# Rewriting a delta-rule and expert kernel as straight-line code with raw keys, a 128-wide state, a second state in PSUM and predicated copies

## The reference, cut to what matters

```
z  = norm(x);  y = layernorm(z; dn_g, dn_b)
q, k, v = split(y @ gates_w + gates_b);  lr = y @ lr_w + lr_b
k  = k / |k|
A  = tril(k k^T, -1) + I;  u = solve_triangular(A, v, lower)      # per sequence, 1024 x 1024
h  = z + ((q k^T) @ (lr * u)) @ out_w + out_b                     # no causal mask
h  = h + relu(layernorm(h; mn_g, mn_b) @ w1 + b1) @ w2 + b2
x1 = x + h
e  = argmax(norm(x1) @ gate_w^T)                                  # 8 experts, one per position
out = x1 + norm(x1) + norm(x1) @ expert_w[e]^T
```

## Time and profile before

| | us |
|---|---|
| median of 3 runs (lowest, highest) | 296.16 (295.07, 334.09) |
| profiled execution, first to last instruction | 293.0 |
| PE busy | 211.6 (72%) |
| DVE busy | 208.1 (71%) |
| ACT busy | 153.6 (52%) |
| POOL busy | 104.6 (36%) |
| chain that ended last, by engine | PE 37%, DVE 35%, ACT 10%, issue 9% |

### The profile page before, as it was taken

The page is one execution under the profiler, slowest core; times in us unless marked ns, Lnnn a source line. Parts: engine busy times, 40 slices in busy tenths (PEclk is TensorE's granted clock), DMA queues, the critical chain, the costliest instruction groups (busy, mean ns, idle before and its releaser), DMA issues.

```text
span 293.0 us, 5160 instructions
## 1 busy us (share of the span) xinstructions
PE 211.6 (72%) x1322; PEld 143.6 (49%) x1322; DVE 208.1 (71%) x743; ACT 153.6 (52%) x466; POOL 104.6 (36%) x167
## 2 busy tenths in 40 slices
PE   0687678540007999999997362989798989897990
PEld 0475466330006888787873241736264544644440
DVE  5599997579993355555553425398989899999785
ACT  2578779630024555555531214275758685766851
POOL 6005455750000000000000503057576766867485
PEclk9979999855555899999999875799999999999997
DMA  5964454512002122222120100000110202010111
GB/s 121 254 220 178 158 233 166 232 67 115 0 1 107 38 110 96 86 110 80 58 112 2 37 36 0 0 1 24 51 33 38 72 2 72 0 38 0 36 36 36
DMA packets 18740, 22.39 MB, mean 76 GB/s; under 512 B 2328, under 2 KB 12576, under 8 KB 18720
## 3 DMA queue, kind: packets, MB, share of 16 engines
q1 hardware_dynamic: 18720, 22.16, 21.3%
HBM read 3.28 MB, written 2.10 MB: 18 GB/s over the span
## 4 chain that ended last, share of the span: by engine, by line
PE 37%; DVE 35%; ACT 10%; issue 9%; SPq 2%; DMA 2%; POOL 1%; DVEq 1%; ACTq 0%
PE ps L1019 8%; PE ps L1166 5%; PE ps L1025 4%; DVE xi L791 4%; DVE st L680 4%; PE ps L1159 4%; DVE prod L784 3%; PE ps L1236 3%; PE ps L1142 3%; ACT sq L464 3%; DVE xi L951 2%; DVE xnT L898 2%; DVE mv L687 2%; DVE lt L943 2%; PE ps L1252 2%
## 5 line engine op out<-in xcount | busy, mean ns | idle before, releaser
L1259 PE MATMUL ps<-ewT,tt 128*128 128x512 f32 x128 | 59.2, 599 | 1.6 <-DVE lt L943 1.4
L631 ACT ACTIVATE gd_all<-ps,oh 128x128 f32<-128x128 f32 x128 | 36.1, 368 | 18.2 <-PE ps L1259 15.7
L414 POOL TENSOR_TENSOR h_all<-h_all,cb 128x512 f32<-128x512 f32 (+1 forms) x8 | 10.2, 1270 | 95.8 <-DVE cb L871 95.8
L1259 PEld LDWEIGHTS ps<-ewT,tt 128*128 128x128 f32 x128 | 22.5, 190 | 27.4 <-issue 17.6
L951 DVE TENSOR_TENSOR xi<-lt,gd_all 128x512 f32<-128x512 f32 x32 | 25.4, 795 | 6.1 <-DVE lt L943 2.8
L230 POOL TENSOR_TENSOR xi<-xi 128x256 f32<-128x256 f32 x31 | 22.5, 726 | 16.0 <-DVE xi L951 16.0
L550 ACT COPY tt<-dT_all 32x128 f32<-32x128 f32 (+1 forms) x32 | 13.0, 407 | 23.2 <-DVE dT_all L796 22.7
L1092 PE MATMUL ps<-tt,gs 32*32 32x32 f32 x128 | 5.0, 203 | 27.2 <-ACT tt L550 26.5
L378 POOL COPY gd_all<-gg 32x128 f32 (+1 forms) x28 | 11.9, 425 | 31.6 <-ACT gg L482 28.6
L824 DVE TENSOR_TENSOR sm<-ps,sm 128x256 f32<-128x256 f32 x32 | 13.0, 421 | 12.9 <-PE ps L1166 12.4
L943 DVE TENSOR_TENSOR lt<-ps,oh 128x512 f32<-128x512 f32 x32 | 21.6, 676 | 0.0
(11 more groups left out here) (127 smaller groups left out, 497.3 us busy)
## 6 DMA issues: line engine op xcount, KB each, us to landing
kv_all<-kv SPq DMA_DIRECT2D x8, 512.0 KB, 3.1
kvs<-kv_all SPq DMA_DIRECT2D x8, 512.0 KB, 2.9
x_all<-in_L_attn_x_dram SPq DMA_DIRECT2D x8, 256.0 KB, 4.8
xnT_all<-xnT SPq DMA_DIRECT2D x8, 256.0 KB, 2.3
g_all<-gg SPq DMA_DIRECT2D x8, 256.0 KB, 2.3
gs<-g_all SPq DMA_DIRECT2D x8, 256.0 KB, 2.4
xns<-xnT_all SPq DMA_DIRECT2D x8, 256.0 KB, 2.4
out_dram<-x_all SPq DMA_DIRECT2D x8, 256.0 KB, 2.3
```

What stands on the lines that cost most here:

```text
L631: last = nc.scalar.activation(ea[b][:, e], ps[:, 4 + 2 * b, e * F:e * F + F], ACT.Copy, scale=oh[s][:, n, e:e + 1])
L1259: nc.tensor.matmul(ps[:, bank, :], zT[s][:, n], ewT[:, EH * half:EH * half + EH, :].rearrange("p e f -> p (e f)"), start=True, stop=True). ...
```

## The change

It does five things.

1. No loops: all tiles are unrolled in program order on each engine, every tile has its own place in SBUF (`kT_all`, `k_all`, `v_all`, `gg_all`, `tt_all`), and the DMAs into and out of the staging buffers go.
2. Raw keys: keys are not divided by their length. The transposed keys come straight from one matmul `wk` x xnT of 512 columns, and `k_` turns them back. The lengths come from the diagonal of the Gram blocks (`nkl`), the elimination works on scaled coefficients (`rd`, `lts`), and v is multiplied by the length in `rv_`.
3. State of 128 columns: `ks` applies S to the keys, `rv_` subtracts, `w_` multiplies by the inverse, `s_` makes k^T w of 128 columns. The second state is summed in PSUM bank 4 over all tiles by `m_`.
4. x1 is not normalized before the gate and the experts: their weights are centred (`cent`, `gwC`, `ewC`), x1 itself is turned, and the factor 1/sigma is applied at the end (`scale`). The outputs are chosen by one copy of the last expert (`default`, ACT) and 7 predicated copies (`pick`, DVE) for each pair of sequences; POOL adds the result (`add_`).
5. The orders are new. b2 is added after stage 1, and h (`h_`) is computed there too; POOL builds part of `tt` and `da` in stage 2.

```diff
-            def both(i, s):
-                diagonals(i, s)
-                plus_b2(i, s)
+        pool.wait_ge(ewT_ready, 1)
+        nc.gpsimd.tensor_tensor(ewT[:], ewT[:], ident[:, :].unsqueeze(1).broadcast_to([P, E, F]),
+                                ALU.add).then_inc(ewI_ready, 1)
+        pool.wait_ge(w_loaded, 16 * 10)
+        for t in range(T):
+            pool.wait_ge(h_ready, t + 1)
+            nc.gpsimd.tensor_tensor(x_all[:, t], x_all[:, t], b2s[:, :].unsqueeze(1).broadcast_to([P, NS, C]),
+                                    ALU.add).then_inc(xb2_ready, 1)
...
+        for t in range(T):
+            kT_(t)
+            if t + 2 < T:
+                root(t + 2)
+            if t + 1 < T:
+                xnT_(t + 1)
+            k_(t)
+            if t + 2 < T:
+                xh_(t + 2)
+            gg_(t)
...
+        nc.vector.reciprocal(rd[:], diagonal(lt)).then_inc(rd_done, 1)
+        nc.vector.tensor_tensor(lts[:], lt[:], rd[:].unsqueeze(1).broadcast_to([P, Q, Q]), ALU.mult).then_inc(elim, 1)
+        nc.vector.tensor_copy(diagonal(xi), rd[:]).then_inc(elim, 1)
...
-            nc.tensor.matmul(ps[:, 6 + n % 2, 0:2 * C], kvs[s][:, n, 0:C], uu[:, n], start=True,
-                             stop=True).then_inc(sm_mm[n][s], 1)
+        def ks(t, n):
+            pe.wait_ge(s_ready, (t - 1) * NS + n + 1)
+            nc.tensor.matmul(ps[:, n, 0:C], kT_all[:, t, n], sm[:, n], start=True, stop=True).then_inc(ks_mm, 1)
+        def w_(t, n):
+            pe.wait_ge(rv_ready, t * NS + n + 1)
+            if n == 0:
+                pe.wait_ge(t12_ready, t + 1)
+            nc.tensor.matmul(ps[:, n, C:2 * C], tt_all[:, t, n], rv[:, n], start=True, stop=True).then_inc(w_mm, 1)
+        def s_(t, n):
+            pe.wait_ge(w_ready, t * NS + n + 1)
+            nc.tensor.matmul(ps[:, n, 2 * C:3 * C], k_all[:, t, n], ww[:, n, 0:C], start=True, stop=True).then_inc(s_mm, 1)
+        def m_(t, n):
+            pe.wait_ge(lrw_ready, t * NS + n + 1)
+            last = nc.tensor.matmul(tiles(4)[:, n], ww[:, n, C:2 * C], k_all[:, t, n], start=t == 0 and n == 0,
+                                    stop=t == T - 1, skip_group_check=True)
...
-            nc.vector.tensor_tensor(ed[b], ps[:, 5 + 2 * b, :].rearrange("p (e f) -> p e f", e=EH),
-                                    oh[s][:, n, EH:E].unsqueeze(2).broadcast_to([P, EH, F]), ALU.mult).then_inc(ed_done[b], 1)
-            nc.vector.tensor_tensor(es[b], ed[b], ea[b], ALU.add).then_inc(sum_done[b], 1)
+        def default(t, pair):
+            act.wait_ge(ex_mm, 4 * t + 2 * pair + 1)
+            earlier(act, added, t - 1)
+            nc.scalar.copy(sel[t % 2][:, 2 * pair:2 * pair + 2], ps[:, 4:6, 0:F]).then_inc(default_set, 1)
+        def pick(t, pair, j):
+            e = j + 1
+            half = e // EH
+            b = 4 + 2 * half
+            n = slice(2 * pair, 2 * pair + 2)
+            if j == 0:
+                dve.wait_ge(mask_ready, t + 1)
+                dve.wait_ge(default_set, 2 * t + pair + 1)
+            else:
+                dve.wait_ge(picked, (E - 1) * (2 * t + pair) + j)
+            if j == 0 or e == EH:
+                dve.wait_ge(ex_mm, 4 * t + 2 * pair + half + 1)
+            nc.vector.copy_predicated(
+                sel[t % 2][:, n], mask[t % 2][:, n, E - 1 - e].unsqueeze(2).broadcast_to([P, 2, F]),
+                ps[:, b:b + 2, (e % EH) * F:(e % EH) * F + F]).then_inc(picked, 1)
+        def tn_(t, of):
+            act.wait_ge(hnb_done, t + 1)
...
+        def experts(t, pair, half):
+            i = 2 * t + pair
+            earlier(pe, picked, (E - 1) * i - (EH if half == 0 else 0))
+            for n in range(2):
+                last = nc.tensor.matmul(ps[:, 4 + 2 * half + n, :], x1T[t % 2][:, 2 * pair + n],
+                                        ewC[:, EH * half:EH * half + EH, :].rearrange("p e f -> p (e f)"),
+                                        start=True, stop=True)
+            last.then_inc(ex_mm, 1)
```

More of the change, by code:

```diff
@@ new lines, in xh_, with xnT_ @@
+            def xh_(t):
+                act.wait_ge(nb_done, t + 1)
+                earlier(act, xT_mm, t - 1)
+                for n in range(2, NS):
+                    last = nc.scalar.activation(xh[t % 2][:, n], x_all[:, t, n], ACT.Identity, bias=nb[:, t, 1, n:n + 1],
+                                                scale=rr[:, t, 1, n:n + 1])
+                last.then_inc(xh_act, 1)
+            def xnT_(t):
+                act.wait_ge(xT_mm, t + 1)
+                nc.scalar.activation(rows(xnT_all[:, t]), ps[:, 0, :], ACT.Identity, bias=dnb, scale=dng).then_inc(xnT_ready, 1)
@@ new lines, in _ @@
+            last.then_inc(tt_first, 1)
+            ya(0)
+            za(0)
+            y64_(0)
+            for t in range(T):
+                if t + 1 < T:
+                    ya(t + 1)
+                w_(t, 0)
+                w_(t, 1)
+                if t + 1 < T:
+                    za(t + 1)
+                w_(t, 2)
+                w_(t, 3)
+                lrw(t, 0)
+                lrw(t, 1)
+                if t + 1 < T:
+                    y64_(t + 1)
+                lrw(t, 2)
+                lrw(t, 3)
@@ new lines, in tT_, with hid_, x1T_ @@
+            def tT_(t):
+                act.wait_ge(tT_mm, t + 1)
+                earlier(act, hid_mm, t - 1)
+                nc.scalar.activation(rows(tT[t % 2]), ps[:, 1, :], ACT.Identity, bias=mnb, scale=mng).then_inc(tT_ready, 1)
+            def hid_(t):
+                act.wait_ge(hid_mm, t + 1)
+                earlier(act, out_mm, t - 1)
+                nc.scalar.activation(rows(hid[t % 2]), ps[:, 2, :], ACT.Relu, bias=b1c).then_inc(hid_ready, 1)
+            def x1T_(t):
+                act.wait_ge(x1T_mm, t + 1)
+                nc.scalar.copy(rows(x1T[t % 2]), ps[:, 1, :]).then_inc(x1T_ready, 1)
@@ L1014, in _ @@
-            pe.wait_ge(kvw_loaded, 16 * 6)
-            def four(bank, lhsT, rhs, ready, step=1):
-                for n in range(NS):
-                    last = nc.tensor.matmul(tiles(bank)[:, n], lhsT(n), rhs(n), start=True, stop=True)
-                last.then_inc(ready, step)
             def turn(bank, src, ready):
@@ new lines, in tT_, with hid_, out_ @@
+            def tT_(t):
+                pe.wait_ge(tn_ready, NS * (t + 1))
+                earlier(pe, x1T_ready, t)
+                turn(1, lambda n: tn[t % 2][:, n], tT_mm)
+            def hid_(t):
+                pe.wait_ge(tT_ready, t + 1)
+                earlier(pe, x1_ready, t)
+                nc.tensor.matmul(ps[:, 2, :], w1s[:], rows(tT[t % 2]), start=True, stop=True).then_inc(hid_mm, 1)
+            def out_(t):
+                pe.wait_ge(hid_ready, t + 1)
+                four(2, lambda n: hid[t % 2][:, n], lambda n: w2s[:], out_mm)
```

1531 lines of the change are left out of this document (633 added, 898 removed).

## The result

| | us |
|---|---|
| changed kernel, median of 4 runs (lowest, highest) | 314.23 (313.64, 314.88) |
| kernel before, same comparison | 296.32 (295.07, 334.09) |
| ratio, 95% interval | 1.062 [1.059, 1.066] |
| profiled span | 311.8 (before 293.0) |

The change made the kernel 6.2% slower; 280 was forecast, with a range of 266 to 302. Of the 32 executions of the kernel before on record, 19 took 295 to 297 us, ten 301 to 302 and three 334 to 336, at mean granted clocks of 0.89 to 0.90, 0.86 to 0.87 and 0.77, so its order does not always keep or get the full clock either, though no trace shows where.

What follows compares the result with a forecast made beforehand. Bounds taken: DVE, ACT and PE together in stage 1, DVE in the elimination, PE in stage 2, PE and DVE in stage 3. Gains of 16.2 and 11.4, losses of 11.8 and 1.7 a stage 3 tile: 280 us, range 266 to 302.

Steps and rivals of the forecast that it cites:

- the tile of stage 2: Stage 2 on PE: a tile falls from 7.87 to 6.85 us, gaining 7.1 us over seven tiles.
- The two waits on ACT: Stage 2: w copies wait behind za and lrw behind y64_ on ACT, each costing PE some 0.3 to 0.4 us.
- the price of 0.89: Price taken from the earlier trace for four 128-column matmuls on PE: 0.89 us.
- The clock rival: Stage 3: waits between matmuls make PE's clock fall, costing 27 us, total 307; chance 0.13.
- Stage 1: Stage 1: a tile takes 4.1 us instead of 5.63, and the elimination's first transpose starts near 44.5.
- Elimination: Between stages 1 and 2: 23.85 us grows by 1.55 of DVE work and 10.2 of POOL hold-up to 35.6.
- the 10.2: Elimination: eight b2 additions on POOL, 1.27 us each, hold DVE up for their whole length.
- The bound of 1.0: Elimination: low bound of POOL's hold-up of DVE, 8 x 0.12 us; as a rival 271 us, chance 0.12.
- Stage 3: Stage 3: first pick after 18.5 us, then tiles of 15.0 us against 13.34, with a 4.6 us chain before first picks.
- The 3.2 us added to the span: Final sum: the median run's excess over the profiled span, taking the forecast span of 277.3 to 280.5 us.

Runs made afterwards that it cites:

- e1: Changed kernel with three extra 512-column matmuls (results unused) on PE directly ahead of stage 2's first w_: 288.1 us, 0.970 of the kernel before.
- e2: Changed kernel with t12 issued ahead of m_ on PE in stage 2, no work added: 289.6 us, four executions, 286.6 to 292.8.
- e4: Changed kernel, stage 3 reordered: both first-pair expert halves ahead of tT_ on PE, default ahead of tn_ on ACT: 307.2 us, 1.034 of the kernel before.
- e6: Changed kernel with four extra 128-column matmuls a tile in stage 2, each alone among the small matmuls: 347.6 us, one execution.
- e7: Changed kernel with four extra 128-column matmuls a tile in stage 2, side by side directly behind w_: 290.6 us, one execution.
- e13: Changed kernel with one extra 512-column matmul ahead of stage 2's first w_, in four executions: 320.4, 286.2, 320.5 and 287.5 us.
- e9: Kernel before, with the second four 32x32 matmuls of ya put between uv and wT_ in stage 2: 299.5 us, one execution.
- e12: Changed kernel with ya's eight 32x32 matmuls split in stage 2, four ahead of w_ and four behind: 293.2, 298.3, 298.6 and 308.0 us.
- e3: Changed kernel with POOL's eight b2 additions moved from the elimination into stage 2, one a tile: 306.8 us, 1.035 of the kernel before.

## Why the prediction was wrong

**The step that failed** is the tile of stage 2: "PE alone would be 6.1 ... I take 6.85 (bounds 6.1 and 7.87)". Its prices were those of rows at clock 1.00, and both bounds too. The change took away a third of the 128-column matmuls, and with them the pair `uv`, `wT_` that stood side by side, and I counted that as a saving alone. It was 11.95 us a tile at 1.2 GHz: 35.7 us over seven tiles. At full clock the step is 7.5 to 7.6 (e1, e2), so 0.7 more than the sum gave. The two waits on ACT were as reckoned, 0.3 each in the mean of six tiles of e1; what was short was the price of 0.89 for four 128-column matmuls. It is the row of a group right behind another such group; behind small matmuls `w_` and `ks` took 1.09 (e1), as `uv` did in the kernel before.

That PE enters stage 2 cold stood in the trace of before, in two stretches that the earlier trace rows leaves out and the prediction did not use: the elimination, and the start of stage 2.

```profile
60.70:86.00 25.30, 1.34 (x7) 0.94 (x5) 24.99 (x119) 1.97 (x6) 2.37 (x1) 0.50 0.13 52
86.00:98.80 12.80, 9.11 (x113) 8.35 (x113) 4.45 (x12) 5.17 (x15) 0.00 (x0) 0.54 0.16 63
```

**The clock rival** named the clock, but with another mechanism and in another place. I looked for the danger where PE would wait between matmuls, in stage 3, and there the clock was 0.96 in the steady part: it fell in two of six tiles and cost 3.4 us in all (88.9 us against 6 x 14.25), not 27. It struck where PE was busy 100%. The busy share was the wrong measure: the rows of before on which I leaned (61% and 0.76, 72% and 0.92, 91% and 1.00) happen to order the same way, but stage 2 of the changed kernel has 100% and 0.50. With the Trainium skill's page "TensorE: Matmul & The Clock Gate" (section "HAM oscillation — how this bites in real kernels") I weighed waits between matmuls only. The long pause here is the elimination, and this case shows that the clock, once down, can stay down for 70 us in which PE waits for nothing.

**Stage 1** was right: the elimination's first transpose at 44.74, forecast 44.5, and a tile 4.17, forecast 4.1.

**Elimination**: 33.9 us, forecast 35.6. The trace agrees with the rule of the Trainium skill, page "SBUF — State Buffer", section "SBUF: two separate sides", that the port pair which the two engines share is held for whole instructions by whichever started first. What it adds is the 12 us in which DVE's next operation went ahead of the waiting addition again and again. Moving the additions away gave 8.4 of the 10.2: each addition put one DVE operation of 0.2 us up to 1.2 or 1.3, so it cost about 1.05 and not its whole 1.27, and 8 x 1.05 is 8.4. The bound of 1.0, from the row of L951, did not hold.

**Stage 3** had the right mechanism, and its total the help of luck: 131.3 for 131.0. DVE is idle 3.4 to 4.6 before each first pick, released by the default copy, and a pick takes 0.44 for 0.42. But the first pick came 21.0 behind the stage's first matmul and not 18.5, at a mean clock of 0.71 (180.4 to 204 us); a tile at full clock takes 14.25 and not 15.0; and the falls of the clock in it added 3.4 us in all. These misses cancel. e4 shows that the order made the wait: with it altered, a tile is under the 13.34 of before.

The 3.2 us added to the span were the distance between two different executions; in every execution on record the time is 1.7 to 2.5 above its own span (313.84 against 311.8).

Put together, the changed kernel at full clock is e1 less its burst: 288.1 - 5.4 = 282.7, against the 280 forecast. All of the miss but 3 us is the clock.

**Still open**: what exactly PE must do for the clock to come back. Shown is that the placing of the same matmuls changes the outcome (e2 in four executions, e6 and e7 in one each), that one program can go either way (e13), and that small gaps can be passed (e9 in one execution, e12 sooner or later in four). Not shown is how often each order would fail. What the chip goes by, no run here tells.

## What to carry to other kernels

A matmul's price holds only at the clock at which it was measured; when a change thins out or rearranges PE's work after a long idle stretch, find in the old trace what PE was doing as the clock rose, and ask whether that group is still there. If it is not, full-size matmuls can be put side by side: here that added no work and gave 27 us of span. Work handed to GpSimd "beside" VectorE was beside it here where VectorE read PSUM (e3), and not where VectorE read two SBUF operands without pause. In a hand-written order, what stands between a late result and the first work of the next tile deserves its own sum, as the 4.6 us chain of stage 3 did.

## What the runs showed of the hardware that was not expected

- PE busy 100% for 70 us at 1.2 GHz, without one rise of the clock; the same matmuls in another order rise within two tiles.
- The same program, with one extra full-size matmul ahead of the first `w_`: 286.2 and 287.5 us in two executions, 320.4 and 320.5 in two others.
- VectorE's operations on two SBUF operands, issued without pause, kept a GpSimd addition of 1.27 us waiting for 12 us, so that it took 13.2; then three pairs of VectorE operations of 0.4 us took 2.5 us each.
- A predicated copy of 128x256 from PSUM with an int32 mask, broadcast over 128 columns, takes 0.44 us, as a tensor_tensor of that shape does (0.42).
